# Score pass of a graph transformer layer: unrolled, with half of the row additions moved from TensorE to VectorE

## The reference

```python
xn = layernorm(x)
z = (xn @ W_s.T)[src] + (xn @ W_t.T)[dst]     # one row per edge
z = where(z >= 0, z, 0.2 * z)
e = z @ W_attn.T                              # the score of an edge
alpha = softmax of e over the edges of equal src
agg = segment_sum(xn[src] * alpha, dst)
x = x + agg @ W_fc.T + b_fc + mixer(xn)       # mixer: k, v normalized per head, dots = k^T v
x = x + moe(layernorm(x))                     # top-1 of 8 experts
```

## Time and profile before

| | us |
|---|---|
| median of 3 runs | 2489.02 |
| lowest, highest | 2488.91, 2490.25 |
| the profiled execution | 2494.62 |
| its span in the trace | 2492.8 |
| of this, score pass, first gather to last weighted sum | 259 to 1344 |

### The profile page before, as it was taken

The page is one execution under the profiler, slowest core; times in us unless marked ns, Lnnn a source line. Parts: engine busy times, 40 slices in busy tenths (PEclk is TensorE's granted clock), DMA queues, the critical chain, the costliest instruction groups (busy, mean ns, idle before and its releaser), DMA issues. The chain is left out here.

```text
span 2492.8 us, 48185 instructions
## 1 busy us (share of the span) xinstructions
PE 2292.8 (92%) x11299; PEld 1672.5 (67%) x11299; DVE 1514.7 (61%) x6003; ACT 902.4 (36%) x3930; POOL 1186.6 (48%) x1218
## 2 busy tenths in 40 slices
PE   0997799999999999999998999999999469999998
PEld 0554466666666666666666899888988436666665
DVE  5444466666666666666664888888888304444443
ACT  0674144343344434334443344444444122222221
POOL 0000677777777777767671343554554212222222
PEclk9997699999999999999998999999999679999999
DMA  5236799899888888988883877777777312222220
GB/s 175 108 127 194 225 277 278 268 279 272 263 259 267 262 263 268 270 260 264 262 265 113 214 240 221 238 222 227 241 227 219 106 63 76 78 78 78 85 71 9
DMA packets 286019, 493.14 MB, mean 198 GB/s; under 512 B 42736, under 2 KB 210210, under 8 KB 285772
## 3 DMA queue, kind: packets, MB, share of 16 engines
q1 hardware_dynamic: 211548, 267.66, 33.9%
q0 software_dynamic: 74352, 224.13, 31.0%
HBM read 370.47 MB, written 126.89 MB: 200 GB/s over the span
## 5 line engine op out<-in xcount | busy, mean ns | idle before, releaser
L701 POOL DMA_INDIRECT pool_mem<-node_tab,pool_mem x592 | 576.5, 974 | 463.0 <-DVE pool_mem L939 263.7
L948 DVE SCALAR_TENSOR_TENSOR x_all<-psum,pool_mem 128x258 f32<-128x258 f32 x784 | 332.6, 424 | 353.5 <-PE psum L839 346.7
L1594 PE MATMUL psum<-x_all,pool_mem 128*128 128x256 f32 x1568 | 360.6, 383 | 0.4 <-DVE pool_mem L1776 0.2
L839 PE MATMUL psum<-pool_mem,ident 128*128 128x258 f32 x1184 | 342.4, 412 | 1.3 <-DMA pool_mem<-node_tab,pool_mem 1.3
L1594 PEld LDWEIGHTS psum<-x_all,pool_mem 128*128 128x128 f32 x1568 | 295.4, 191 | 41.2 <-issue 1.1
L834 PE MATMUL psum<-x_all 32*128 32x258 f32 x1568 | 279.9, 432 | 6.7 <-DMA x_all<-proj_t 6.7
L839 PEld LDWEIGHTS psum<-pool_mem,ident 128*128 128x128 f32 x1184 | 203.6, 192 | 119.6 <-issue 100.5
L745 ACT ACTIVATE x_all<-x_all,neg_max 128x8 f32<-128x8 f32 x98 | 29.6, 302 | 658.6 <-DVE neg_max L960 658.6
L1405 POOL DMA_INDIRECT x_all<-node_tab,edges x196 | 200.4, 1023 | 120.8 <-issue 74.4
L2382 PE MATMUL psum<-x_all,xn_all 128*128 128x256 f32 x1024 | 223.1, 380 | 7.7 <-ACT xn_all L2405 7.7
L701 POOL DMA_INDIRECT x_all<-node_tab,pool_mem x192 | 185.4, 966 | 83.9 <-issue 74.1
(11 more groups left out here) (246 smaller groups left out, 3655.4 us busy)
## 6 DMA issues: line engine op xcount, KB each, us to landing
x_all<-kept_rows SPq DMA_DIRECT2D x98, 768.0 KB, 4.8
kept_rows<-pool_mem SPq DMA_DIRECT2D x74, 768.0 KB, 5.8
kept_rows<-x_all SPq DMA_DIRECT2D x24, 768.0 KB, 6.7
x_all<-in_L_ffn_w_dram SPq DMA_DIRECT2D x16, 1024.0 KB, 8.2
node_tab<-pool_mem SPq DMA_DIRECT2D x49, 258.0 KB, 2.5
x_all<-proj_t SPq DMA_DIRECT2D x392, 32.2 KB
x_all<-edge_rows SPq DMA_DIRECT2D x98, 128.0 KB
pool_mem<-node_tab,pool_mem POOLq DMA_INDIRECT x592
```

Of the source, the lines that this page charges most:

```text
L701: g.indirect_dma_start(source_rows(r, u, ZW + D), None, node_tab, bass.IndirectOffsetOnAxis(ap=w_idx[r][:, u:u + 1], axis=0)).then_inc(s_i ...
L839: pe.matmul(psum[:, Z_BANK[u % GROUPS_W], 0:ZW], ident[:, :], source_rows(r, u, ZW), start=False, stop=True).then_inc(s_z, 1)
L948: v.scalar_tensor_tensor(out=dot_w[:, u % 4, :], in0=psum[:, Z_BANK[u % GROUPS_W], 0:ZW], scalar=0.0, in1=attn_w, op0=ALU.max, op1=ALU.mul ...
L1594: pe.matmul(psum[:, bank, 0:D], wide_picked[:, HALF * (k % 2) + u, :], row, start=(odd == 1 and n == 0), stop=(n == HALF - 1)).then_inc(s_ ...
```

## The change

The score pass is written without loops, so every semaphore value, index and address is a constant. In it:

- Tiles come in four pairs. For pairs 0 and 2 TensorE still does both steps (`expand`, `add_rows`, L831 and L841). For pairs 1 and 3 it only expands the destination rows. VectorE then adds the source rows from the ring (`add_row`, L961) into `zsum` in SBUF, and weighs that sum in a second instruction (`weigh_row`, L965), whose two inputs lie in SBUF. For pairs 0 and 2 VectorE weighs the bank as before (`weigh_sum`, L954).
- The order of all steps is new on TensorE, VectorE and ScalarE. A bank comes free at `weigh_sum` or `add_row` (`s_zr`).
- Gathers read their indices directly in `edges`. The copies to `w_idx` are gone, and so is the copy of scores (L954 of before): scores are written in `score_all` at once.
- Destinations are stored and brought as bytes (`dst_rows`), modulo 256, for which the first block gets two more casts, and three small steps on `group_id`.
- The waits no longer carry a second semaphore increment (`hold`).

Six of eight tiles keep their rows, before and after.

```diff
-    edge_rows = nc.dram_tensor("edge_rows", (1, ET * P), F32, kind="Internal").ap()
+    dst_rows = nc.dram_tensor("dst_rows", (1, ET * P), U8, kind="Internal").ap()
...
-        w_idx = [m.take(HALF).bitcast(I32) for _ in range(RING)]
         attn_w = m.take(ZW)
+        zsum = m.take(4, ZW)
...
+        BY_VECTOR = (1, 3)
+        BY_TENSOR = (0, 2)
...
-                    def sum_z(k, h, r, pair):
-                        first = 2 * pair
-                        j = first // GROUPS_W
+                    def expand(k, pair):
+                        h, j = k % 2, pair // 2
                         if pair == 0:
                             wait(pe, s_hotT, k + 1)
...
+                            wait(pe, s_zr, HALF * k + u - 3)
+                            mm = pe.matmul(psum[:, Z_BANK[q], 0:ZW], hot_T[h][rows_q, j * P:(j + 1) * P], t_win[rows_q, h, :], start=True,
+                                           stop=(pair in BY_VECTOR), tile_position=(q * GROUP_ROWS, 0))
+                            if pair in BY_VECTOR:
+                                mm.then_inc(s_z, 1)
...
+                    for k in range(HALVES - 1):
+                        expand(k, 3)
+                        expand(k + 1, 0)
+                        add_rows(k + 1, 0)
+                        first_part(k)
+                        expand(k + 1, 1)
+                        expand(k + 1, 2)
+                        add_rows(k + 1, 2)
+                        second_part(k)
...
+                    def add_row(k, u):
+                        r = k % RING
+                        wait(v, s_z, HALF * k + u + 1)
+                        wait(v, s_in[r][u // GATHERS], 16 * GATHERS * (k // RING + 1))
+                        v.tensor_tensor(zsum[:, u // GROUPS_W * 2 + u % 2, :], psum[:, Z_BANK[u % GROUPS_W], 0:ZW], source_rows(r, u, ZW), ALU.add).then_inc(s_zr, 1)
+
+                    def weigh_row(k, u):
+                        wait(v, s_zr, HALF * k + u + 1)
+                        v.scalar_tensor_tensor(out=dot_w[:, u % 4, :], in0=zsum[:, u // GROUPS_W * 2 + u % 2, :], scalar=0.0, in1=attn_w, op0=ALU.max, op1=ALU.mult,
+                                               accum_out=score_at(k, u)).then_inc(s_added, 1)
...
+                    for k in range(HALVES):
+                        more = k + 1 < HALVES
+                        add_row(k, 6)
+                        add_row(k, 7)
+                        mix(k, 0, 2)
+                        weigh_row(k, 6)
+                        weigh_row(k, 7)
+                        mix(k, 2, 3)
+                        half_top(k)
+                        if k > 1:
+                            merge(k - 2)
+                        if more:
+                            weigh_sum(k + 1, 0)
+                            weigh_sum(k + 1, 1)
...
+                        if k + 2 < HALVES:
+                            hot(k + 2)
+                        if k % 2 == 0 and k > 0:
+                            mix_values(k // 2 - 1)
```

More of the change, by code:

```diff
@@ L647, in graph_transformer_kernel @@
         turn_w = dot_w.rearrange("p a c -> p (a c)")[:, 0:NT * HALF].rearrange("p (m u) -> p m u", u=HALF)
[L648 removed]
+        dst_row = [m.take(GROUP_EDGES // 4).bitcast(U8) for _ in range(2)]
         hot_T = [m.take(GROUP_EDGES) for _ in range(2)]
@@ L831, in sum_z @@
                             q = u % GROUPS_W
                             rows_q = slice(q * GROUP_ROWS, (q + 1) * GROUP_ROWS)
-                            wait(pe, s_sc, HALF * k + u - 3)
-                            pe.matmul(psum[:, Z_BANK[q], 0:ZW], hot_T[h][rows_q, j * P:(j + 1) * P], t_win[rows_q, h, :], start=True, stop=False,
-                                      tile_position=(q * GROUP_ROWS, 0))
-                        for u in range(first, first + 2):
+                            wait(pe, s_zr, HALF * k + u - 3)
@@ L1055, in _ @@
-                    dve.leave(STEP_PASSES)
-                    for k in range(LAST_STEP, HALVES - 1):
-                        step(k, k, k // 2)
-                    merge(HALVES - 3, 1)
-                    lo_hots(HALVES - 1, 1, 0)
-                    lo_hots(HALVES - 1, 1, 1)
-                    hi_hots(HALVES - 1, 1)
-                    running_max(HALVES - 1, 1)
+                    hot(0)
+                    hot(1)
+                    weigh_sum(0, 0)
+                    weigh_sum(0, 1)
@@ new lines, in _ @@
+                    add_row(0, 2)
+                    add_row(0, 3)
+                    weigh_sum(0, 4)
+                    weigh_sum(0, 5)
+                    weigh_row(0, 2)
+                    weigh_row(0, 3)
+                    for k in range(HALVES):
+                        more = k + 1 < HALVES
[11 more added lines that the diff above has]
+                            weigh_sum(k + 1, 1)
+                        mix(k, 3, 5)
+                        lo_hots(k, 0)
+                        mix(k, 5, 6)
+                        if more:
+                            add_row(k + 1, 2)
+                            add_row(k + 1, 3)
+                        mix(k, 6, 7)
+                        running_max(k)
+                        hi_hots(k)
+                        mix(k, 7, 8)
+                        if more:
+                            weigh_sum(k + 1, 4)
+                            weigh_sum(k + 1, 5)
+                        mix(k, 8, 9)
+                        lo_hots(k, 1)
+                        mix(k, 9, 10)
+                        if more:
+                            weigh_row(k + 1, 2)
+                            mix(k, 10, 11)
+                            weigh_row(k + 1, 3)
+                            mix(k, 11, 12)
+                        if k + 2 < HALVES:
+                            hot(k + 2)
+                        if k % 2 == 0 and k > 0:
+                            mix_values(k // 2 - 1)
@@ L1194, in _ @@
-                    for k in range(HALVES - 2, HALVES):
-                        keep(k, k % RING)
+                            wait(sp, s_in[r][g], 16 * GATHERS * (k // RING + 1))
+                        sp.dma_start(kept_rows[k, :, :, :], taken[r][0][:, :, ZW:ZW + D]).then_inc(s_kst[r], 16)
+                    fetch(0)
+                    fetch(1)
+                    for k in range(HALVES):
+                        keep(k)
+                        if k + 2 < HALVES:
+                            fetch(k + 2)
```

275 lines of the change are left out of this document (109 added, 166 removed).

## The result

The changed kernel takes 2431.34 us (median of 4 runs, 2430.24 to 2437.75), beside 2489.64 us for the kernel before in the same series: a ratio of 0.9771, 95% interval 0.9753 to 0.9788. The forecast was 2433.7 us, in a range of 2400 to 2486. The profiled execution took 2430.24 us, its span is 2428.4.

The account below looks back on a forecast made before the run. GpSimd's gathers bound the pass: 10.0 us plus 0.45 of holds a half. Ending at 1287.9 instead of 1344.0 gains 56.1 us, less 0.8 for new steps: profiled 2439.3, median 5.6 lower, 2433.7 us; range 2400 to 2486.

Parts of the forecast that it names:

- The bound: Score pass: TensorE, full before, gives way to GpSimd's gather issue, 10.0 us a half; pace 10.45 us with lengthened gathers.
- TensorE and VectorE: Score pass, work per half: TensorE falls from 10.96 to 9.26 us, VectorE rises from 7.3 to 8.6 us.
- The clock: TensorE's granted clock should hold at 1.00 with waits, as in an earlier stretch busy 53.1 of 60 us.
- The holds: Gathers lengthened by VectorE instructions with two SBUF inputs, `weigh_row` included: 0.45 us a half, from 0.22 to 0.76.
- The sum of squares: Gather delay scales with squared VectorE instruction lengths, starts falling at random: 1.27 becomes 2.52, scaled from the observed 0.22 us.
- Start: Without VectorE's index copies, GpSimd's first gather begins at 258 instead of 259.05 us.
- End: Last gather starts at 1280.9, last weighted sum ends at 1287.9 us, then an unchanged tail of 11 us.
- (a): Rival: gathers lose 0.22 us a half or less, pace 10.0 to 10.2, 2390 to 2411 us; chance 0.10.
- (c): Rival: VectorE, working in order, becomes the bound: 22.9 us a pair of halves, 2533 us; chance 0.12 for slower.
- Transfers: Score pass data movement stays hidden with little to spare, at a pace of 10.2 us a half already kept up.
- Unrolling gives nothing: Writing out the score pass's loops has no effect, as TensorE was busy in 200 of 200 us.

Follow-up runs that it names:

- seven_gathers: Changed kernel without every eighth gather, tile 7 using tile 6's rows (partly wrong results): 2354.47 us, ratio 0.9440.
- one_pair: Changed kernel with pair 1's additions given back to TensorE, only pair 3 added by VectorE: 2421.67 us, ratio 0.9723.
- no_pair: Changed kernel with all four pairs added by TensorE, still in the new order and without loops: 2487.81 us, ratio 0.9983.
- one_input: Changed kernel with `weigh_row` replaced by an instruction of one SBUF input, leaving out the attention weights for four tiles of eight: 2428.88 us, ratio 0.9745.
- filler: Changed kernel with two unused multiplications of zeros added per half on TensorE: 2412.00 us, ratio 0.9674.
- two_holds: Changed kernel with two unused VectorE instructions of two SBUF inputs added per half: 2446.47 us, ratio 0.9818.
- lo_hots_later: Changed kernel with VectorE's `lo_hots(k, 1)` moved behind the last `weigh_row` of the half: 2441.7 us, ratio 0.9793.
- unrolled: Kernel before the change with only the score pass's loops written out for all engines: 2502.10 us, ratio 1.0039.
- two_reduces: Changed kernel with two unused VectorE reductions of one SBUF input added per half, the control of `two_holds`: 2437.15 us, ratio 0.9776.
- one_filler: Changed kernel with one unused multiplication of zeros per half on TensorE, ahead of the half's first expansion: 2423.9 us, ratio 0.9733.

## Why the prediction was right, and where not

**The bound** was right: TensorE leaves it, GpSimd's issue takes its place, VectorE stays under it. Pace 10.45 predicted, 10.31 measured. `seven_gathers` shows it on the chip, and `one_pair` and `no_pair` that the additions do it.

**TensorE and VectorE.** 9.26 us for a half was predicted and cannot be read from a waiting engine. It was busy in 852 of 950 us, 90%, and 9.26 / 10.31 is 90%, but that proves little: `seven_gathers` gives TensorE the same work, at a clock of 0.89, and was busy for 886.11 / 950 x 9.40 = 8.8 us of a half. So 9.26 was too much, and the agreement is partly luck. VectorE: 8.6 predicted, 157.03 / 200 x 10.31 = 8.1 measured. `add_row` took 0.42 us, as taken, but starts 0.35 us after the one ahead, the lower end of what I gave. A group of 276 of them was busy for 104.5 us, 0.38 us each, so four cost 1.5 us of the 1.6 taken. Most of the miss lies elsewhere: a `weigh_row` took 145.6 / 368 = 0.40 us where I kept 0.43 for every weighing, and the rest wasn't followed.

**The clock** was wrong. I had it stay at 1.00 since a stretch with 88% busy had 1.00. In the changed kernel the same stretch, with the same matmuls and 52.59 of 60 us busy, shows 0.91, and the pass 0.87. The step failed as it took one row for a rule. No cost of it shows, as TensorE wasn't the bound: at 0.87 its gaps are only smaller. Whether it raised the extra is the open question above.

**The holds** were right in kind and too large. 0.45 us for a half was predicted, 32.6 / 98 = 0.33 measured, some 12 us in all. The instructions were right: `weigh_row` does hold gathers, with 35 of 124 long ones. The sum of squares took starts as falling at random, scaled once; but the starts aren't random, and the extra moves from 12 to 47 us by what stands where. In `one_input` the holds of `weigh_row` went away and the extra stayed as it was. I also took every two-input instruction to hold whatever starts beside it, and `hot` to hold nothing. So a term of this kind has no point value before the order is run, only its two ends, and my 0.22 to 0.76 held it for the changed kernel, while `filler` came out below, at 0.13.

The Trainium skill, "SBUF — State Buffer", section "Who interferes with whom": that two SBUF inputs contend and one, outside VectorE's two-port modes, doesn't, agrees with 90 long gathers against 3 in `two_holds` and its control. `hot`, with its one tensor of bytes, held 19 of 19 in `lo_hots_later`; whether it runs in such a mode no trace shows.

**Start.** I had GpSimd begin at 258 without the index copies; it began at 259.1, as before. The other kernels without the copies begin between 257.4 and 259.2, and `unrolled`, which has them, at 258.4: what the copies cost is too small to see here. Rows of GpSimd after, against the earlier trace rows:

```profile
259.11 1.66 POOL L707 DMA_INDIRECT pool_mem<-node_tab,edges  x1 [256.55 <-issue]
261.08 1.31 POOL L707 DMA_INDIRECT pool_mem<-node_tab,edges  x1 [0.30 <-issue]
```

**End.** The last gather was expected at 1280.9 and starts at 1268.6: 12 us early, nearly all by the holds. From there to the last weighed sum I had 7.0 us; it took 12.0. The timeline of the three engines:

```profile
1268.59 1.19 POOL L707 DMA_INDIRECT pool_mem<-node_tab,edges  x1 [0.30 <-issue]
...
1274.15 1.14 PE L841 MATMUL psum<-pool_mem,ident 128*128 128x258 f32 x4
...
1278.53 0.69 DVE L1015 TENSOR_TENSOR x_all<-psum,x_all 128x512 f32<-128x512 f32 x1
1279.14 0.75 DVE L961 TENSOR_TENSOR pool_mem<-psum,pool_mem 128x258 f32<-128x258 f32 x2
...
1280.15 0.42 DVE L965 SCALAR_TENSOR_TENSOR x_all<-pool_mem 128x258 f32<-128x258 f32 x1
...
1294.41 0.27 DVE L998 SCALAR_TENSOR_TENSOR tab_sum<-tab_sum,x_all,psum 128x49 f32<-128x49 f32 x1 [3.81 <-PE psum L855]
```

The rows are used 5.6 us after the last gather's start, as said. But the last pair's `add_row` stands behind an even half's norm steps and L1015 on VectorE, and waits for these. I had counted only the two adds and weighs, and not what stands ahead of them in the row. The tail to the last merge is 13.8 us for 11. So: 12.3 us better at the last gather, 5.0 and 2.8 us worse behind it. The last merge went from 1355.01 to 1294.41, by 60.6 us, where I had 55.3. The span fell by 64.4, and the other 3.8 us, in the blocks behind, stay unexplained. So the profiled executions differ by 9 us more than forecast, and the medians only by 3 (58.3 for 55.3): the profiled execution of before lies 5.6 us above its median, that of after 1.1 below. The forecast is closer than its steps were: misses of 12, 8 and 4 us and the place of two executions largely cancel.

**Rivals.** (a), holds of 0.22 or less, came out for `filler` only, with 12.3 / 98 = 0.13 us. (c), VectorE as the bound: it waited 140.0 us for TensorE ahead of L961 alone, so it was far from it. The sum given for (c) was also wrong: its terms come to 24.9 us a pair of halves, not 22.9, and so to 12.4 us for a half. **Transfers** stayed hidden, at a share of 0.89; no gather waited for a store until one in eight was taken away.

**Unrolling gives nothing** was wrong in size. By itself it costs some 10 us on the old order. What it costs in the new order wasn't tried, since the new order was not built with loops.

## What to carry to other kernels

Read an issuing engine by the distance between the starts of its instructions and not by its busy time: 144 of 200 us hid a queue that was 91% full, and it was the next bound. When an engine stops being the bound, stop moving work off it: here the first pair gave 66 us (2487.8 to 2421.7), the second took 10 back. Where many small holds between two engines set the pace, try a few placings of the holding instructions and compare the sum of what the held ones take beyond their shortest time; here this sum told the time of nine kernels to within 4 us, as the issuing engine never paused in them.

## What the hardware showed beyond that

- An indirect gather of 128 rows that starts while VectorE runs an instruction with two SBUF inputs ends 0.82 us after that instruction, in `lo_hots`, `hi_hots`, `weigh_row` and the added line alike, unless it starts within 0.03 to 0.04 us of the instruction's start: in the changed kernel all 120 later ones were held and none of the 26 earlier ones. Beside one SBUF input of float32 (`one_input`, `two_reduces`), or one in PSUM and one in SBUF (`add_row`), it takes its 0.95 us. Beside `hot`, with one input of bytes, it was held in 19 of 19 cases.
- More work on TensorE made a kernel 19 us faster. `filler` at 2412.0 us is the fastest version that computes the reference, 0.9674 of the kernel before.
- The granted clock in one stretch of the first block was 0.91 in the changed kernel's execution and 1.00 in that of the kernel before, at 52.6 and 53.1 busy us of 60. It doesn't follow the busy time: the same stretch had 1.00 at 52.2 us in `one_filler` and 0.93 at 53.3 us in `seven_gathers`.
- Straight code of the score pass was 0.39% slower than the same code in loops, with TensorE busy all the time in both.
